# Attention on 32-row and 32-column pieces of the array, with a folded score weight in the second attention

## What is computed

```
x = x + xattn(layernorm(x), ctx)      # 16 heads of 32; softmax over the 257 context tokens; then Wo, bo
x = x + attn(layernorm(x))            # one head of 512: q = xWq+bq, k = xWk+bk, v = xWv+bv
                                      # scores = q k^T / sqrt(512), causal,
                                      # softmax over the WHOLE 32x32 matrix of a batch element
x = x + ffn(layernorm(x))             # 512 -> 2048 -> 512 with binarized weights alpha*sign(w), exact gelu
```

## Time and profile before

| | us |
|---|---|
| median of three runs | 2809.39 |
| the profiled execution | 2811.9 |
| its span, first to last instruction | 2810.2 |
| TensorE busy | 2685.3 (96%) |
| VectorE busy | 1712.2 (61%) |
| ScalarE busy | 1275.9 (45%) |
| GpSimd busy | 773.4 (28%) |
| instructions on TensorE | 17468 weight loads, 17468 matmuls |

### The profile page before, as it was taken

One profiled execution on the slowest core, in us unless ns is written; L12 is line 12 of the kernel. 1 busy time (PEld: TensorE's weight loads), 2 busy tenths in 40 slices (PEclk: granted clock), 3 DMA queues, 4 the chain that ended last, 5 costly groups with the idle time before them and its releaser, 6 DMA issues. The chain is left out here.

```text
span 2810.2 us, 51774 instructions
## 1 busy us (share of the span) xinstructions
PE 2685.3 (96%) x17468; PEld 1589.4 (57%) x17468; DVE 1712.2 (61%) x3492; ACT 1275.9 (45%) x2826; POOL 773.4 (28%) x1530
## 2 busy tenths in 40 slices
PE   7999999999999999999999999668999998999999
PEld 4455555555555555555555555345666666666666
DVE  7566656555565555655556555476566666566664
ACT  4355554454544544445444454234344443444344
POOL 2233433333333333333333333112111111111110
PEclk9999999999999999999999999879999999999999
DMA  3243433333333333333333333330000000000000
GB/s 139 96 96 95 104 86 87 88 79 89 86 86 88 79 88 86 85 89 79 88 87 85 90 79 80 74 107 21 16 16 16 15 30 15 15 15 15 20 19 16
DMA packets 336307, 185.75 MB, mean 66 GB/s; under 512 B 282352, under 2 KB 302832, under 8 KB 335728
## 3 DMA queue, kind: packets, MB, share of 16 engines
q1 hardware_dynamic: 336240, 184.90, 25.8%
HBM read 109.06 MB, written 8.65 MB: 42 GB/s over the span
## 5 line engine op out<-in xcount | busy, mean ns | idle before, releaser
L680 DVE TENSOR_TENSOR e_lo<-e,e_hi 128x1024 f16<-128x1024 f32 x128 | 156.8, 1225 | 414.3 <-ACT e_hi L610 414.3
L597 ACT ACTIVATE v_hi<-psum 128x512 f16<-128x512 f32 x256 | 152.8, 597 | 529.8 <-PE psum L764 529.8
L764 PE MATMUL psum<-c_hi,xWk_hi 128*128 128x512 f16 x1024 | 388.1, 379 | 2.3 <-PEq L136 2.3
L764 PE MATMUL psum<-xWv_hi,c_hi 128*128 128x512 f16 x1024 | 388.1, 379 | 0.0
L764 PE MATMUL psum<-xWv_lo,c_hi 128*128 128x512 f16 x1024 | 388.1, 379 | 0.0
L764 PE MATMUL psum<-xWv_hi,c_lo 128*128 128x512 f16 x1024 | 388.1, 379 | 0.0
L764 PE MATMUL psum<-c_lo,xWk_hi 128*128 128x512 f16 x1024 | 388.1, 379 | 0.0
L764 PE MATMUL psum<-c_hi,xWk_lo 128*128 128x512 f16 x1024 | 388.1, 379 | 0.0
L604 ACT ACTIVATE e<-psum,neg_max 128x257 f32<-128x257 f32 x512 | 236.3, 474 | 281.0 <-DVE neg_max L662 281.0
L673 DVE SCALAR_TENSOR_TENSOR v_lo<-psum,v_hi 128x512 f16<-128x512 f32 x256 | 177.1, 692 | 222.0 <-ACT v_hi L597 221.7
L118 POOL TENSOR_TENSOR c_lo<-ctx_raw,c_hi 128x1024 f16<-128x1024 f32 x128 | 271.9, 2124 | 12.9 <-ACT c_hi L347 10.3
(11 more groups left out here) (193 smaller groups left out, 5890.2 us busy)
## 6 DMA issues: line engine op xcount, KB each, us to landing
ctx_raw<-in_ctx_main SPq DMA_DIRECT2D x128, 512.0 KB, 3.3
xs<-in_x SPq DMA_DIRECT2D x8, 1024.0 KB, 5.6
v_rep<-v_last_rows SPq DMA_DIRECT2D x512, 16.0 KB, 1.8
xb<-in_x SPq DMA_DIRECT2D x16, 512.0 KB, 3.6
out<-res_out SPq DMA_DIRECT2D x32, 256.0 KB, 2.0
ffn_raw<-in_w_t SPq DMA_DIRECT2D x11, 512.0 KB, 3.6
late_raw<-in_late_w SPq DMA_DIRECT2D x4, 1024.0 KB, 4.8
res<-in_w_t SPq DMA_DIRECT2D x5, 512.0 KB, 4.1
```

The source lines that it names most:

```text
L597: nc.scalar.mul(v_hi[u][:, t, :], v_bank(t), W_UNSCALE).then_inc(v_hi_done, 1)
L680: nc.vector.tensor_tensor(e_lo[:, :, :], e[:, :, 0:S], e_hi[:, :, :], ALU.subtract).then_inc(e_lo_done, 1)
L764: mm = nc.tensor.matmul(bank, a, b, start=(n == 0), stop=(n == len(steps) - 1))
```

## The change

The layout of the cross-attention turns: a bank holds head `h` of every group, and the 32 partitions of block `g` belong to group `g`. It has these parts:

- `score`: no block-diagonal tile. Each head's queries (32 features x 32 tokens, in `qb`) are a weight of 32 rows and 32 columns, and its keys (32 rows, 257 columns) stream; the result goes to partitions 32 g to 32 g + 31 of bank `h`. 3 passes x 16 heads = 48 matmuls, in an order in which four that follow one another differ in their rows, in their columns and in their bank.
- `outputs`: for each head, the head's 32 columns of `pT` are the weight (128 rows), its 32 value columns stream; 4 heads x 2 halves x 3 passes x 4 groups = 96 matmuls, four neighbours on four column groups. VectorE gathers the result in one instruction, GpSimd copies `qb` in two.
- The waits ahead of `score` are set before the last matmul of the values before it (`await_scores`).
- Wo's rows are loaded in the new order, in four DMAs (`load_output_weight`); the other late weights come in four DMAs each, too.
- The second attention's scores (xWq + bq)(xWk + bk)^T are rearranged: M = Wq Wk^T is computed once, so that for each group only xM + (Wk bq)^T is projected (two banks instead of four) and multiplied with x; the term that depends on the row, x (Wq bk), is taken by VectorE with two row sums for each group (`row_terms`) and goes into the mask with the constant bq bk. The preparation transposes Wq and Wk on TensorE (`turn`), multiplies them and makes the vectors (`fold_weights`), before and in the first round.

```
@@ cross_queries, ScalarE @@
-                nc.scalar.mul(vl[:, :].rearrange("p (h g d) -> p g h d", h=4, g=KC),
-                              v_last_bank.rearrange("p (g h d) -> p g h d", h=4, g=KC),
-                              W_UNSCALE).then_inc(vl_done, 1)
+                nc.scalar.mul(vl[:, :], v_last_bank, W_UNSCALE).then_inc(vl_done, 1)
@@ cross_attention @@
-        bd_hi = sb_in(ctx, "bd_hi", [P, KC, HPG, L], F16)
-        bd_lo = sb_in(ctx, "bd_lo", [P, KC, HPG, L], F16)
+        qb_hi = sb_in(ctx, "qb_hi", [P, KC, L], F16)
+        qb_lo = sb_in(ctx, "qb_lo", [P, KC, L], F16)
...
-        out_bank = psum[:, 3, :].rearrange("p (g n) -> p g n", g=KC)
+        out_bank = psum[:, 3, 0:KC * 32].rearrange("p (h d) -> p h d", h=HPG)
...
+            def load_output_weight():
+                by_slot = late_w[0:1].rearrange("o (h d) (g n) -> g d (o h) n", h=HPG, g=KC)
+                for g in range(KC):
+                    sp.dma_start(late_raw[32 * g:32 * g + 32, 0, :].rearrange("p (h n) -> p h n", h=HPG),
+                                 by_slot[g]).then_inc(late_landed, 16)
...
-                for h in range(HPG):
-                    rows = slice(32 * h, 32 * h + 32)
-                    nc.gpsimd.tensor_copy(bd_hi[rows, :, h, :],
-                                          heads_hi[rows, :, bass.ds(b * L, L)]).then_inc(bd_ready, 1)
-                    nc.gpsimd.tensor_copy(bd_lo[rows, :, h, :],
-                                          heads_lo[rows, :, bass.ds(b * L, L)]).then_inc(bd_ready, 1)
+                for qb, heads in ((qb_hi, heads_hi), (qb_lo, heads_lo)):
+                    nc.gpsimd.tensor_copy(qb[:, :, :], heads[:, :, bass.ds(b * L, L)]).then_inc(qb_ready, 1)
...
-                for h in range(HPG):
-                    rows = slice(32 * h, 32 * h + 32)
-                    nc.vector.tensor_tensor(o_sum[rows, :, :], out_bank[rows, :, 32 * h:32 * h + 32],
-                                            last_part[rows, :, :], ALU.add).then_inc(o_sum_done, 1)
+                nc.vector.tensor_tensor(o_sum[:, :, :], out_bank, last_part[:, :, :],
+                                        ALU.add).then_inc(o_sum_done, 1)
...
+                for n, (a, w) in enumerate(steps):
+                    if scores_next and n == len(steps) - 1:
+                        await_scores(*scores_next)
+                    mm = nc.tensor.matmul(v_bank(t), a, w, start=(n == 0), stop=(n == len(steps) - 1))
...
+            def await_scores(i, u):
+
                 b = i * 4 + u
-                pe.wait_ge(bd_ready, 2 * HPG * (b + 1))
+                pe.wait_ge(qb_ready, 2 * (b + 1))
                 pe.wait_ge(k_col, 2 * (i * 2 + u // 2 + 1))
                 pe.wait_ge(k_lo_done, KC * (i * 2 + u // 2 + 1))
                 past(pe, e_done, KC * b)
-                past(pe, o_sum_done, HPG * (b - 1))
-                for g in range(KC):
-                    mm = run(psum[:, g, 0:S + 1],
-                             [(q[:, g, :, :].rearrange("p h l -> p (h l)"), k[u // 2][:, g, u % 2, 0:S + 1])
-                              for q, k in passes(bd_hi, bd_lo, kT_hi, kT_lo)])
+                past(pe, o_sum_done, b - 1)
+
+            def score(i, u):
+                for n, (q, k) in enumerate(passes(qb_hi, qb_lo, kT_hi, kT_lo)):
+                    for turn in range(KC):
+                        for h in range(HPG):
+                            g = (h + turn) % KC
+                            rows, outs = slice(32 * h, 32 * h + 32), slice(32 * g, 32 * g + 32)
+                            mm = nc.tensor.matmul(psum[outs, h, 0:S + 1], q[rows, g, :],
+                                                  k[u // 2][rows, g, u % 2, 0:S + 1], start=(n == 0),
+                                                  stop=(n == 2))
...
-                for g in range(KC):
-                    cols = slice(g * P, (g + 1) * P)
-                    mm = run(out_bank[:, g, :], [(p[:, g * ST + t, :], v[:, t, cols]) for t in range(ST)
-                                                 for p, v in passes(pT_hi, pT_lo, v_hi[u % 2], v_lo[u % 2])])
+                for h in range(HPG):
+                    steps = [(p, v, t) for t in range(ST)
+                             for p, v in passes(pT_hi, pT_lo, v_hi[u % 2], v_lo[u % 2])]
+                    for n, (p, v, t) in enumerate(steps):
+                        for g in range(KC):
+                            outs, cols = slice(32 * g, 32 * g + 32), slice(g * P + 32 * h, g * P + 32 * h + 32)
+                            mm = nc.tensor.matmul(out_bank[outs, h, :], p[:, h * ST + t, outs], v[:, t, cols],
+                                                  start=(n == 0), stop=(n == len(steps) - 1))
@@ token_stages, ScalarE @@
+                eng.wait_ge(s["consts_landed"], 16 * 6)
+                nc.scalar.mul(bias_hi[:, :], bqk_col[:, :], W_SCALE).then_inc(s["bias_hi_done"], 1)
+                for i in range(2 * KC):
+                    eng.wait_ge(s["turn_ps"], KC * (i // KC + 1))
+                    nc.scalar.copy(turned(late_hi, i), turn_bank(i)).then_inc(s["turn_hi_done"], 1)
...
+                for m in range(KC):
+                    nc.scalar.mul(late_hi[:, 1, m, :], turn_bank(m), W_UNSCALE).then_inc(s["fold_hi_done"], 1)
@@ token_stages, VectorE @@
+                for t in range(T):
...
+                    nc.vector.tensor_tensor_reduce(
+                        out=val[:, :], in0=xn[:, t, :], in1=row_w[:, :], op0=ALU.mult, op1=ALU.add,
+                        scale=1.0, scalar=0.0, accum_out=row_term[:, t:t + 1]).then_inc(s["row_term_done"], 1)
...
                     low_T(s["x2T_hi_done"], x2T_hi, x2T_lo, s["x2T_lo_done"], n)
+                    if isinstance(n, int) and n == 0:
+                        fold_products()
+                    row_terms(n)
@@ token_stages, TensorE @@
+            def turn(w):
+                for c in range(KC):
+                    if w == 2:
+                        pe.wait_ge(s["turn_lo_done"], c + 1)
+                    for k in range(KC):
+                        cols = slice(k * P, (k + 1) * P)
+                        mm = run(turn_bank(c)[:, cols], [(part[:, w, k, c * P:(c + 1) * P], ident_h[:, :])
+                                                         for part in (late_hi, late_lo)])
+                    mm.then_inc(s["turn_ps"], 1)
+            def fold_weights():
+                pe.wait_ge(s["turn_lo_done"], 2 * KC)
+                for m in range(KC):
+                    cols = slice(m * P, (m + 1) * P)
+                    mm = run(turn_bank(m), [(q[:, 1, e, cols], k[:, 2, e, :]) for e in range(KC)
+                                            for q, k in passes(late_hi, late_lo, late_hi, late_lo)])
...
                     transposes(n, s["norm2_done"], s["t2_ps"])
...
-                    for r in range(4):
-                        hi, lo = late["sWq" if r < 2 else "sWk"]
+                    for r in range(2):
+                        hi, lo = late["sM"]
...
+            pe.wait_ge(s["ident_h_done"], 1)
+            turn(1)
+            turn(2)
             rounds(pe, one)
```

More of the change, by code:

```diff
@@ L512, in quad @@
             def quad(i, late):
-                if late:
+                if i == 0:
+                    load_output_weight()
+                elif late:
                     load_late(i)
@@ L555, in last_token @@
                 b = i * 4 + u
-                pool.wait_ge(bd_ready, 2 * HPG * (b + 2 if more else b + 1))
+                pool.wait_ge(qb_ready, 2 * (b + 2 if more else b + 1))
                 pool.wait_ge(e_done, KC * (b + 1))
                 pool.wait_ge(rep_landed[u % 2], 16 * HPG * (i * 2 + u // 2 + 1))
-                past(pool, o_sum_done, HPG * b)
+                past(pool, o_sum_done, b)
                 nc.gpsimd.tensor_tensor(last_part[:, :, :], v_rep[u % 2][:, :, :],
@@ L575, in _ @@
             spread(0, 0)
-            pool.wait_ge(bd_ready, 2 * HPG)
+            pool.wait_ge(qb_ready, 2)
             last_keys(0, 0)
@@ L816, in step @@
                 if more:
-                    values(b + 1, (u + 1) % 4, 1)
+                    values(b + 1, (u + 1) % 4, 1, (i + u // 3, (u + 1) % 4))
             for m in range(KC):
@@ L821, in _ @@
             values(0, 0, 0)
-            values(0, 0, 1)
+            values(0, 0, 1, (0, 0))
             for u in range(4):
@@ L1208, in maxima @@
                         out=sc[rows, :, :], in0=sc_bank[rows, :, BT * b:BT * b + BT], scalar=SCALE,
-                        in1=mask[rows, :].unsqueeze(1).to_broadcast([BT, T, BT]), op0=ALU.mult,
+                        in1=mask_row[rows, :, :], op0=ALU.mult,
                         op1=ALU.add).then_inc(s["sc_done"], 1)
@@ L1423, in one @@
                 if front:
+                    if isinstance(n, int) and n == 0:
+                        fold_weights()
+                        pe.wait_ge(s["fold_vec_done"], 1)
                     transposes(n, s["norm2_done"], s["t2_ps"])
@@ L1427, in one @@
```

(14 more changed lines are left out.)

137 lines of the change are left out of this document (100 added, 37 removed).

## The result

After the change the kernel takes 2619.86 us, the median of four runs (2614.30, 2615.53, 2624.19, 2633.09), against 2809.86 us before in the same comparison: a ratio of 0.933 with a 95% interval of 0.929 to 0.937, 190 us saved. The forecast was 2769 us and 2620 to 3010. The profiled execution took 2624.19 us, its span 2622.4.

The account below looks back on a forecast made before the run. Both stages were taken as bound by TensorE's stream of matmuls. Cross-attention +19.5 us, token groups -78.6 and the first group's preparation +19 gave -40, so 2769 us against a median of 2809.39; range 2620 to 3010.

Parts of the forecast that it names:

- The small pieces: Cross-attention scores and outputs on 32x32 pieces: 144 pairs at 15 ns, 2.16 us per element instead of 2.66.
- The switches: Cross-attention: four changes of the array's cut per element, 0.163 us each, 0.65 us together.
- Round it, at no cost: Cross-attention: query copies, output gathering, split weight DMAs and moved waits stay hidden beside busy TensorE, adding no time.
- The fold in the groups: Token stage: 48 of 96 projection matmuls go, 5.24 us off each of 15 groups, -78.6 us.
- The first round: Token stage's start: preparing the folded weight delays the first weight piece 26 us, 7 come back, +19 us.
- Sum: Whole kernel: 19.5 - 78.6 + 19 = -40 us, giving 2769 us.
- The faster entry: Rival, cross-attention: pieces on different groups run at once, entering in half of 15 ns; -0.93 us per element, 2631 us; chance 0.15.
- The sequencer step: Rival, cross-attention: each small matmul costs one 27.9 ns instruction step, +2.01 us per element, 3006 us; chance 0.27.

Follow-up runs that it names:

- the earlier place: The changed kernel with GpSimd's staging of the next token group put only after VectorE has the attention weights: 2614.8 us (2598.15 to 2624.65).

## Why the prediction was wrong, point by point

- **The small pieces: the step that failed.** The forecast took 15 ns a pair, the middle of what a pair takes after a stall, though it had bounded the price from below at under 5. Measured: 9.1 ns for the scores and 8.3 for the outputs, 48 x 9.1 + 96 x 8.3 = 1.24 us instead of 2.16. That is 0.92 us per element, 118 us. The rows after a stall show single pairs on the full array; in the small pieces the pairs of different pieces start side by side, sixteen in about 0.12 us, as the row at 900.77 and the next show, while the outputs of one column group still stand 25 to 33 ns apart. The forecast had the overlap too small.
- **The switches** were sized too high. The element's -0.95 = 1.24 + four switches - 2.66, which leaves 0.47 us for the four, 0.12 each, where the forecast took 0.163; two further ones cost 0.08 each. Another 23 us.
- **Round it, at no cost:** held. The cross-attention has no new wait on a semaphore, and the element is a bare row of matmuls.
- **The fold in the groups:** the 5.24 us came off as forecast and no VectorE step became last. From the first to the last of the 14 waits for gelu_lo a group went from 59.46 to 53.12 us, though, 6.34 less. The 1.1 us beyond the forecast are the clock: after the wait the transposes ran slowed in 14 of 14 groups before (1.24 to 1.49 us from the first to the last start, 0.76 at full clock), in 8 of 14 after. Slowed matmuls cost 2.0 us a group before and 1.0 after; over 15 groups some 16 us. Why the shorter group keeps the clock in mostly every second round was not found.
- **The first round:** against the sum of xb, the first weight piece came 25.1 us later (36.5 instead of 11.4 us; forecast 26) and the fourth 19.8 us later (forecast 19). Held.
- **Sum.** The forecast's -40, less 118, 23 and 16, plus about 10 for the stalled turn that no step had, is -187 us; the span shrank by 187.8.
- **The rivals.** The faster entry, at 7.5 ns a pair 2631 us, is what happened; it had a chance of 0.15. That its element (-0.93 us) comes so near to the measured one (-0.95) is partly luck: its pairs were too cheap and its switches too dear, by nearly the same. The sequencer step of 27.9 ns is refuted: 16 pairs, 32 instructions, start in 0.12 us. The Trainium skill's floor of about 25 ns from start to start (TensorE: Matmul & The Clock Gate, on the 56 ns gap) was given beside it. On the full array this trace agrees with it: the fold's one-column matmuls start 25 to 30 ns apart.

```profile
1731.28 0.17 PE L1442 MATMUL psum<-bias_hi,late_hi 128*128 128x1 f16 x1
1731.31 0.16 PE L1442 MATMUL psum<-bias_lo,late_hi 128*128 128x1 f16 x1
1731.34 0.16 PE L1442 MATMUL psum<-bias_hi,late_lo 128*128 128x1 f16 x1
1731.36 0.16 PE L1442 MATMUL psum<-bias_hi,late_hi 128*128 128x1 f16 x1
```

  The outputs agree on each column group, 25 to 33 ns; for the pieces of the array together it does not hold: 8 to 9 ns, because they run side by side. What the Trainium skill says of a change of the tiling mode (TensorEngine Tiling (Array Packing), Key Properties), that it drains TensorE, agrees with a price per switch, at 0.08 to 0.12 us.

## What to carry to other kernels

Work that fills a quarter of the array or less is worth splitting into pieces even where that means four times the instructions: price such a pair at 8 to 9 ns and each way in or out at 0.1 us, and leave their order free as long as neighbours are on different column groups: with two groups at a time instead of four the pair was 12.5 ns. Then look at what the many cheap instructions need: a loop whose turn no longer stays in the instruction store stops the engine just where its instructions are short, and the spread of the times from run to run is the sign of it; a few instructions ahead of the loop can settle it. And where a wait of TensorE ends with a VectorE instruction, compare that instruction's duration there with its duration elsewhere, and look at what GpSimd does at that moment: its work can be moved to where nothing waits for the VectorE instruction beside it.

## What the runs showed that was not expected

- A turn of 1584 TensorE instructions stalls or not by where it starts: 2.8 to 3.5 us from start to start at its top and 3.1 to 5.4 us after its 22nd pair, 8 to 10 us in all with the lower clock behind it, in up to 6 of 30 turns. Moved by 96 instructions none of eight runs shows it, moved by 256 two of four. With full-array pairs a refetched turn costs 0.7 us.
- 48 score pairs listed piece by piece take 1.05 us where piece after piece would take 3.5: a busy piece does not stop the pairs behind it, and matmuls start out of the program's order.
- Output pairs of one column group start 25 to 33 ns apart in either order; the price of 8 ns is four groups at once.
- VectorE's gelu_lo takes 2.55 us instead of 0.42 beside GpSimd's sum over 128x1024 in float32, and xn 1.24 instead of 0.55 beside its casts; these were nearly all of a 3.6 us wait of TensorE in each group, since with the staging moved behind the values the longest wait for gelu_lo is 0.8 us (1.2 with the earlier place).
- After that wait TensorE ran at a lower granted clock (0.57 over the 4 us shown) in 14 of 14 groups before the change and in 8 of 14 after (for one of them in part); without the wait in none.
